# A GRU update on one core: reset and update gates of half the nodes from one matmul of 128 output rows, their sigmoids in quarters

## The reference

```
gi = a @ w_ih.T + b_ih            # split into i_r, i_z, i_n
gh = feat @ w_hh.T + b_hh         # split into h_r, h_z, h_n
r = sigmoid(i_r + h_r);  z = sigmoid(i_z + h_z)
n = tanh(i_n + r * h_n)
feat = (1 - z) * n + z * feat
```

## Time and profile before

| | us |
|---|---|
| median of three runs | 7337.82 |
| lowest and highest | 7335.02, 7353.33 |
| profiled execution | 7338.52 |
| its span, first to last instruction | 7336.8 |
| mean granted TensorE clock | 0.827 of full |

### The profile page before, as it was taken

The page is one execution under the profiler, slowest core; times in us unless marked ns, Lnnn a source line. Parts: engine busy times, 40 slices in busy tenths (PEclk is TensorE's granted clock), DMA queues, the critical chain, the costliest instruction groups (busy, mean ns, idle before and its releaser), DMA issues. The chain is left out here.

```text
span 7336.8 us, 96109 instructions
## 1 busy us (share of the span) xinstructions
PE 4935.3 (67%) x39375; PEld 2538.1 (35%) x39375; DVE 4431.9 (60%) x7733; ACT 3720.7 (51%) x2634; POOL 3759.0 (51%) x3297
## 2 busy tenths in 40 slices
PE   0110238774444458999889989899988377676678
PEld 0110114432222224555545555455554211111123
DVE  9889977654334445554455545445444599999700
ACT  0000009975555455665556656566655177777401
POOL 0017777777777755688764888638870000000230
PEclk9755559987777779999999999999999576767799
DMA  9920028884443355766557756466654233334398
GB/s 412 428 73 0 0 67 277 258 229 149 158 154 145 141 198 173 239 212 221 189 173 228 241 186 231 149 224 229 224 190 142 97 143 155 153 146 158 141 418 363
DMA packets 344782, 1415.02 MB, mean 193 GB/s; under 512 B 129310, under 2 KB 182836, under 8 KB 314516
## 3 DMA queue, kind: packets, MB, share of 16 engines
q1 hardware_dynamic: 159676, 1138.67, 42.6%
q10 hardware_dynamic: 79672, 239.96, 8.7%
q0 software_dynamic: 104992, 30.24, 3.2%
HBM read 1008.21 MB, written 400.36 MB: 192 GB/s over the span
## 5 line engine op out<-in xcount | busy, mean ns | idle before, releaser
L582 PE MATMUL ps_all<-ring,T 128*64 128x448 f16 x32928 | 3324.9, 363 | 840.3 <-ACT ring L745 686.1
L582 PEld LDWEIGHTS ps_all<-ring,T 128*64 128x64 bf16 x32928 | 1923.3, 113 | 2226.1 <-issue 798.5
L744 ACT ACTIVATE ring<-ring 128x3136 uint16<-128x3136 uint8 x502 | 1410.4, 2810 | 1676.8 <-DVE t L1077 861.5
L479 POOL DMA_INDIRECT R<-in_edge_attr,eid x1568 | 1893.2, 1207 | 664.9 <-issue 477.0
L447 POOL DMA_INDIRECT mat_d<-cT,idxT x1563 | 1685.3, 1078 | 965.4 <-ACT cT L686 489.2
L745 ACT ACTIVATE ring<-ring 128x3136 uint16<-128x3136 uint8 x502 | 1405.9, 2801 | 0.0
L1115 DVE SCALAR_TENSOR_TENSOR R<-R,ring 128x784 f32<-128x784 uint16 x392 | 363.3, 974 | 811.1 <-DMA csum_d<-R 727.4
L1671 POOL DMA_INDIRECT sg<-seg_d,endI x49 | 57.8, 1179 | 1208.9 <-POOLq L199 1194.3
L536 PE MATMUL ps_all<-ident,R 128*128 128x128 f32 x448 | 108.3, 422 | 809.2 <-DVE R L835 809.2
L1614 PE MATMUL ps_all<-ad,ones 3*128 3x384 bf16 (+1 forms) x686 | 320.7, 467 | 343.4 <-ACT ps_all L1584 342.7
L1590 ACT ACTIVATE L<-ps_all,bias 128x384 f32<-128x384 f32 (+1 forms) x686 | 425.9, 621 | 148.7 <-PE ps_all L1614 145.4
(11 more groups left out here) (372 smaller groups left out, 3887.3 us busy)
## 6 DMA issues: line engine op xcount, KB each, us to landing
ring<-mat_d SPq DMA_DIRECT2D x784, 784.0 KB
C<-csum_d SPq DMA_DIRECT2D x98, 3136.0 KB, 15.5
mat_d<-ring SPq DMA_DIRECT2D x98, 1568.0 KB, 39.6
csum_d<-R ACTq DMA_DIRECT2D x196, 784.0 KB
seg_d<-R ACTq DMA_DIRECT2D x32, 1568.0 KB
msg_d<-t ACTq DMA_DIRECT2D x196, 128.0 KB
R<-in_edge_attr,eid POOLq DMA_INDIRECT x1568
mat_d<-cT,idxT POOLq DMA_INDIRECT x1563
```

The lines of the kernel that those rows point to most:

```text
L479: pool.indirect_dma_start(slab[n % 2][:, c, 0:FA], None, attr, bass.IndirectOffsetOnAxis(eid[:, at:at + 1], 0)).then_inc(s_at[n % 2], 16)
L582: mm = pe.matmul(accs[h * D:(h + 1) * D, j, 0:GW], lhsT, ring[:, n % 6, h * HQ + j * GW:h * HQ + (j + 1) * GW], start=first, stop=True, sk ...
L744: act.activation(to[:, 0, :], two[:, 0, :], ACT.Copy)
```

## The change

The r and z weights are neighbours in `Wg[h]` (columns 0 to 127), so one matmul now makes both gates of one half: bank `4 * (j % 2) + h` holds r of half h in rows 0 to 63 and z in rows 64 to 127. The two n parts (k = 2, 3) stay as they were. Eight matmuls per group become six. The sigmoids must bring the results to the rows where VectorE reads them, so each of the two becomes two of 64 rows, four per group; half 0's r goes from rows 0 to 63 to rows 64 to 127, half 1's z from rows 64 to 127 to rows 0 to 63, the other two stay in their rows. Semaphores, buffers and VectorE's work are the same.

```
-                        for k in range(4):
+                        own = [G[:, h * HQ + j * GW:h * HQ + (j + 1) * GW] for h in range(2)]
+                        for h in range(2):
+                            pe.matmul(bank(4 * (j % 2) + h)[:, 0:GW], Wg[h][:, 0:2 * D], own[h], start=True, stop=True)
+                        for k in range(2, 4):
                             for h in range(2):
                                 rows = slice(D, P) if h == 0 else slice(0, D)
-                                mm = pe.matmul(bank(4 * (j % 2) + k)[rows, 0:GW], Wg[h][:, k * D:(k + 1) * D],
-                                               G[:, h * HQ + j * GW:h * HQ + (j + 1) * GW], start=True, stop=True)
+                                mm = pe.matmul(bank(4 * (j % 2) + k)[rows, 0:GW], Wg[h][:, k * D:(k + 1) * D], own[h],
+                                               start=True, stop=True)
...
                         for k in range(2):
-                            sg = act.activation(RZ[j % 2][:, k, :], bank(4 * (j % 2) + k)[:, 0:GW], ACT.Sigmoid,
-                                                bias=gb[:, k:k + 1])
+                            rows = slice(k * D, (k + 1) * D)
+                            for h in range(2):
+                                to = slice(D, P) if h == 0 else slice(0, D)
+                                sg = act.activation(RZ[j % 2][to, k, :], bank(4 * (j % 2) + h)[rows, 0:GW], ACT.Sigmoid,
+                                                    bias=gb[rows, k:k + 1])
                         sg.then_inc(s_sg, 1)
```

## The result

The changed kernel takes 7383.06 us in the median of nine runs (7369.99 to 7409.44); the kernel before, run beside it, 7349.95 us in nine (7329.18 to 7367.98), where the three runs known to the prediction had a median of 7337.82. The ratio is 1.0050, with a 95% interval of 1.0038 to 1.0062: by the ratio 37 us slower, 28 to 46. The forecast was 26.4 us and 7364 us.

What follows compares the result with a forecast made beforehand. The prediction took the serial ScalarE-VectorE handover in the GRU updates as the bound. Sigmoids 25.2 plus matmuls 1.2 made 26.4 us, raising the profiled 7338.5 to 7364.9; the median being 0.7 lower, it forecast 7364 us, range 7352 to 7375.

Steps and rivals of the forecast that it cites:

- The place: GRU update ending each of four steps: ScalarE and VectorE hand over without overlap, so exposed time there counts one for one.
- The ring of ScalarE and VectorE: In the update, sigmoids(j+1) waits for after(j-1) because RZ has two buffers; groups 2 to 6 forecast every 6.97 us.
- group 0 hidden: Opening of each update: group 0's extra sigmoid time fits before pair 1 can start, by 0.8 us on ScalarE.
- The sigmoid's term: Update, six groups of seven in four steps: two more sigmoids at 0.525 us each, 1.05 us a group, 25.2 us.
- Rival C: Sigmoids and wide matmuls: crossing halves stops overlap (48 x 0.63 = 30.2 us), wide passes pay 4.8; 7373 us; 13%.
- Rival B: Additional sigmoids run at the copy's pitch of 0.43 us: 20.6 plus 1.2 us, 7360 us; 10%.
- Matmuls, 1.2 us: TensorE in groups 0 and 1: trips between 128 and 64 output rows cost 0.3 us per step, 1.2 us in all.
- The sum is the same 3.0 us: Gate matmuls of a group: six stream as many columns as eight did, so fewer instructions save nothing.
- Time by columns, not rows: ScalarE's sigmoids: time goes by columns, hardly by rows, so 64x448 was forecast at about 630 ns.
- Rival A: Sigmoids: time goes by rows too, four take as long as two, only TensorE's 1.2 us left; 7339 us; 4%.
- Rival D: Ring-piece transfers and POOL's gathers get ahead during the longer update; half the delay comes back; 7351 us; 8%.

Runs made afterwards that it cites:

- the third buffer: A third RZ buffer, added to the kernel before (ratio to before 0.9971) and to the changed kernel (ratio to before 0.9972).
- The straight additional sigmoids: Kernel before plus two more 128-row sigmoids in groups 2 to 6, into a spare tile nobody reads; ratio 1.0030.
- straight halves: Kernel before with its matmuls kept, each sigmoid split into two of 64 rows that stay in their rows; timed again, ratio 1.0052 from three runs.

## Why the prediction was off in size

- *The place.* Right. The ring of ScalarE and VectorE in groups 1 to 6, group 0 hidden (0.80 us of idle time left, forecast 1.1), updates as the only stretch that grows: shown by the table and by the third buffer, which takes the cost of the settled groups away.
- *The sigmoid's term, "Two more instructions cost 2 x 0.525 = 1.05 us".* This step failed. It measured 1.39 us, 33.4 in all for the forecast 25.2. The pitch of 0.525 us was read off two sigmoids, and a tanh, that all work from row 0 on; four instructions with a change of rows between each two start 0.64 us apart, and the change takes the overlap from the pair that was there, too: 3 x 0.64 + 0.63 - 1.16 = 1.39. The straight additional sigmoids show that 1.05 is the right price for two more instructions on the same rows, and nothing more. The text named 0.63 us, "no overlap at all", as the upper end, and then chose "the row of the same function" without asking what else the two instructions of that row had in common. The trace of before holds one place that shows it, the copies of an earlier phase. These are the first two of three in a row (rows 64 to 127, 896 and 448 columns), then all three (the last copies 448 columns from rows 0 to 63 to rows 0 to 63; the row names the shape of the first alone):

```profile
567.19 1.35 ACT L714 ACTIVATE G<-ps_all 64x896 f32<-64x896 f32 x2 [0.55 <-PE ps_all L565]
...
567.19 1.90 ACT L714 ACTIVATE G<-ps_all 64x896 f32<-64x896 f32 x3 [0.55 <-PE ps_all L565]
```

  The copy at other rows adds 1.90 - 1.35 = 0.55 us, its whole duration of 0.54 and a little more; each of the seven that stay in their rows adds 0.43.
- *Rival C* had the lost overlap, for a wrong reason: it put it on "Crossing the halves", which costs nothing (7.07 us a group crossing and straight), and it multiplied 48 added instructions by 0.63, 30.2 us, leaving out what the old ones lose. Its 4.8 us for the wide passes were not there. That its sum of 35.0 meets the updates' 35.3 is luck. *Rival B's* pitch of 0.43 was not there either: straight sigmoids add 0.53 each.
- *Matmuls, 1.2 us.* Too small, though for the reason given, the trip between 128 and 64 rows. The term counts three switches in each opening, and three are there, but a switch costs 0.17 us where the text had 0.20 for there and back: 0.5 us an update, 2 us in all. "The sum is the same 3.0 us" is shown by the kernel with all gates wide. The rule of the Trainium skill, "TensorEngine Tiling (Array Packing)", section Key Properties, that a change of tiling mode drains TensorE, agrees with this trace in kind; its size here is 0.17 us.
- *Time by columns, not rows.* Right: 628 ns for 64 x 448. Rival A falls. The Trainium skill, "ScalarE: Activation LUTs", section What ACT_TABLE_LOAD costs, gives an overlap of 93 ns back to back without a condition; the runs show 0.10 us for activations that begin at the same rows and none between sigmoids where rows change.
- *Rival D, absorption.* Half of the delay was to come back, which would leave 18 us; the interval begins at 28. By stretches, straight halves have updates 33.4 us longer and contractions 5.5 us longer, the changed kernel has the contractions 7.4 us shorter. The contractions of single executions scatter by 20 us, so a small return stays open.
- *The level.* Part of the distance between 7364 and 7383 is no step of the change: the kernel before itself came out at 7349.95 over nine runs, 12 us above the three at hand. This is what carried the time out of the range: with the updates' 35.3 us in place of 26.4 the forecast would have been 7373 us, inside 7352 to 7375, with a ratio of 1.0048.

## What to carry to other kernels

Before an instruction is split, look at whether its neighbours overlap and what they have in common: on ScalarE a split by rows cost the added instructions and the overlap of those already there. If it must be split, put the pieces that read the same rows and write the same rows next to each other. In the experiments with the matmuls of before this brought back 0.24 us of 1.39 a group; the changed kernel could not use it, as each two of its four sigmoids differ in the rows read or in the rows written. And where two engines hand over on one ring, first ask for one more buffer: it made the updates of the kernel before 24 us shorter and hid the change's settled cost.

## What the runs showed of the hardware

- Two activations in a row overlapped by 0.10 us where both the rows read and the rows written begin at the same partition, also when one has 64 rows and the next 128. Two sigmoids that read PSUM did not overlap when either begins elsewhere (0.64 us from start to start for a duration of 0.63; 0.55 for 0.54 without a bias). The bank read and the plane of RZ written change in the overlapping pairs too, so they are not what matters.
- The rows of the bias can decide too: a tanh from row 0 on, which reads no PSUM, overlapped by 0.10 us with a sigmoid that read PSUM rows 64 to 127 without a bias, and not at all with one that also took its bias from these rows. Why is open.
- Reading 64 rows and writing the other 64 costs ScalarE nothing: 2.31 us for four sigmoids with and without it.
- At the full granted clock TensorE loads f32 weights ahead of time within 128-row matmuls and within pairs of 64-row ones, at 0.375 us a pass of 448 columns in both; from one to the other it does not, 0.17 us each time.
